# A decoder layer on one core: GpSimd makes the gate's sigmoid and its sum with the experts' bias, behind the second norm's scale

## What is computed

```python
def _moe(x, gate, expert_bias, w1, w2, w3, shared_w1, shared_w2, shared_w3):
    scores = jax.nn.sigmoid((xt @ gate.T).astype(jnp.float32))
    _, sel = jax.lax.top_k(scores + expert_bias[None, :], TOP_K)
    top_scores = jnp.take_along_axis(scores, sel, axis=1) * ROUTE_SCALE
    ...                        # each token times its two scores, through its two experts
    hs = jax.nn.silu(xt @ shared_w1.T) * (xt @ shared_w3.T)
    out = hs @ shared_w2.T
    out = out.at[token_idx].add(out_r)

x = x + _L0_attn_ref(_layernorm(x), ...)                # 16 heads of 16, each token's own heads
x = x + _L0_xattn_ref(_layernorm(x), ctx_2048, ...)     # 16 heads, 2048 keys, fake quantisation
x = x + _L0_ffn_ref(_layernorm(x), ...)                 # 8 experts, the best 2 of each token
```

## Time and profile before

| | |
|---|---|
| median of 3 runs | 1011.39 us (1009.79 to 1011.78) |
| the profiled execution | 1009.28 us, of which the span (first to last instruction) is 1007.5 |
| busy: VectorE, GpSimd, ScalarE, TensorE | 910.5, 748.0, 733.1, 722.3 us |
| mean granted clock of TensorE | 0.859 |
| VectorE's sigmoid L1166, 16 times | 13.2 us |
| VectorE's sum with the bias L1168, 16 times | 27.7 us |
| GpSimd idle ahead of L481, for VectorE's `hs_max` | 52.2 us, 16 times |

### The profile page before, as it was taken

The page is one execution under the profiler, slowest core; times in us unless marked ns, Lnnn a source line. Parts: engine busy times, 40 slices in busy tenths (PEclk is TensorE's granted clock), DMA queues, the critical chain, the costliest instruction groups (busy, mean ns, idle before and its releaser), DMA issues.

```text
span 1007.5 us, 21210 instructions
## 1 busy us (share of the span) xinstructions
PE 722.3 (72%) x7072; PEld 398.6 (40%) x7072; DVE 910.5 (90%) x1841; ACT 733.1 (73%) x989; POOL 748.0 (74%) x728
## 2 busy tenths in 40 slices
PE   6965766777677768687777777686868777777674
PEld 4543222344343434343444434343434444343243
DVE  3896967999999999999999999999999999999942
ACT  2633756878877888787777778788878878787842
POOL 6689988979797979797897979797979889710000
PEclk9986786989997989888888979798988889797955
DMA  6011795999899999999998999999999989999971
GB/s 238 1 43 47 131 168 105 173 153 184 169 183 172 157 174 159 167 173 172 166 173 161 180 157 192 170 158 174 169 158 172 175 163 169 158 195 163 192 147 31
DMA packets 574018, 156.01 MB, mean 155 GB/s; under 512 B 567251, under 2 KB 571862, under 8 KB 573526
## 3 DMA queue, kind: packets, MB, share of 16 engines
q1 hardware_dynamic: 573910, 154.67, 86.7%
HBM read 9.93 MB, written 2.10 MB: 12 GB/s over the span
## 4 chain that ended last, share of the span: by engine, by line
DVE 45%; issue 24%; PE 19%; ACT 4%; DMA 2%; SPq 2%; POOL 2%; DVEq 0%; POOLq 0%; ACTq 0%
DVE score L1134 30%; PE ps_score L1458 7%; PE ps L1316 6%; DVE gate L1168 3%; ACT prob L824 2%; PE ps_score L1316 2%; SPq L423 2%; DVE exp_bias L1144 2%; DVE early L1184 2%; DMA prob_t<-prob 2%; ACT queries L806 1%; DVE gate L1166 1%; DVE q_parts L1117 1%; PE ps_pv L1488 1%; PE ps L1437 1%
## 5 line engine op out<-in xcount | busy, mean ns | idle before, releaser
L1134 DVE TENSOR_SCALAR_CACHE_REDUCE score<-ps_score,q_neg 128x1024 f32<-128x1024 f32 x512 | 636.2, 1278 | 17.0 <-PE ps_score L1458 15.5
L824 ACT ACTIVATE prob<-score,exp_bias 128x2048 uint16<-128x2048 f32 x256 | 511.1, 1997 | 11.6 <-DVE exp_bias L1144 9.3
L1458 PE MATMUL ps_score<-keys,queries 128*128 128x512 bf16 x1024 | 351.8, 444 | 195.0 <-DVE score L1134 156.3
L1458 PEld LDWEIGHTS ps_score<-keys,queries 128*128 128x128 bf16 x1024 | 75.4, 104 | 370.7 <-DVE score L1134 306.0
L527 POOL TENSOR_TENSOR product<-hs_exp,v_tok 128x1024 f32<-128x1024 f32 x64 | 148.5, 2342 | 18.0 <-ACT hs_exp L789 17.9
L534 POOL TENSOR_TENSOR product<-product 128x512 f32<-128x512 f32 x128 | 158.9, 1263 | 0.0
L527 POOL TENSOR_TENSOR product<-qk_rot 128x1024 f32<-128x1024 f32 x64 | 149.6, 2350 | 0.3 <-POOL qk_rot L520 0.2
L545 POOL TENSOR_TENSOR product<-product 128x512 f32<-128x512 f32 x64 | 82.4, 1288 | 5.9 <-POOL product L534 5.9
L877 ACT ACTIVATE routed_both<-normed,routed_gate 128x256 bf16<-128x256 f32 x128 | 57.1, 496 | 37.8 <-DVE routed_gate L1179 37.8
L1488 PE MATMUL ps_pv<-prob_t,values 128*32 128x128 f16 x4096 | 73.0, 227 | 11.0 <-DMA prob_t<-prob 10.9
L1488 PEld LDWEIGHTS ps_pv<-prob_t,values 128*32 128x32 f16 x4096 | 62.0, 101 | 40.4 <-issue 40.4
(11 more groups left out here) (124 smaller groups left out, 1125.8 us busy)
## 6 DMA issues: line engine op xcount, KB each, us to landing
prob_t<-prob SPq DMA_TRANSPOSE x256, 4.7
prob_t<-in_w SPq DMA_DIRECT2D x3, 1024.0 KB, 4.8
x_in<-in_x SPq DMA_DIRECT2D x16, 128.0 KB, 3.1
score<-in_cond_t SPq DMA_DIRECT2D x4, 512.0 KB, 6.6
out<-x_out SPq DMA_DIRECT2D x16, 128.0 KB, 2.5
w_qkv<-in_w_qkv SPq DMA_DIRECT2D x1, 768.0 KB, 4.3
early<-in_w_kv SPq DMA_DIRECT2D x1, 512.0 KB
w_s<-in_w_s SPq DMA_DIRECT2D x3, 128.0 KB
```

What stands on the lines that cost most here:

```text
L824: act.activation(prob[:, s, :].bitcast(U16), score[:, s, :], ACT.Exp, bias=exp_bias[:, s:s + 1], scale=-1.0, accum_out=prob_sum[:, t.par, ...
L1134: dve.tensor_scalar(score[:, s, HALF * i:HALF * i + HALF], ps_score[:, score_slot(t.count(H, h), i)].rearrange("p b k -> p (b k)"), q_neg[ ...
L1458: mm = pe.matmul(ps_score[:, score_slot(n, i), b, :], queries[:, t.par, h // 2, h % 2, :], keys[:, h // 2, k0:k0 + KEYS], start=True, stop ...
```

## The change

Both instructions leave VectorE's `choose`. A new function of GpSimd's, `gate_sums`, makes them: it waits for ScalarE's tanh and, from the second tile on, for the last step of the `choose` before; it makes the sigmoid as a tensor_scalar and the sum as a tensor_tensor (it was a scalar_tensor_tensor). It is called in GpSimd's body directly behind the second norm's `ln_scale(1, n)`. VectorE's `choose` begins with the wait for the second count of `gate_chain`, ahead of `max`. The order of all other instructions stays.

```diff
             def gate_sums(t):
+                sig, biased = gate[:, 0, :], gate[:, 1, :]
+                pool.wait_ge(gate_tanhed, t.count(1, 1))
+                pool.sem_inc(settled, 1)
+                if (due := t.due(6)) is not None:
+                    pool.wait_ge(gate_chain, due)
+                    pool.sem_inc(settled, 1)
+                pool.tensor_scalar(sig, gate_tanh[:], 0.5, 0.5, ALU.mult, ALU.add).then_inc(gate_chain, 1)
+                pool.wait_ge(gate_chain, t.count(6, 1))
+                pool.sem_inc(settled, 1)
+                pool.tensor_tensor(biased, sig, b_expert[:], ALU.add).then_inc(gate_chain, 1)
...
                     ln_scale(1, n)
+                if m.exists():
+                    gate_sums(m)
                 if a.exists():
                     fold_8(0, a)
...
             def choose(t):
-                dve.wait_ge(gate_tanhed, t.count(1, 1))
-                dve.tensor_scalar(sig, gate_tanh[:], 0.5, 0.5, ALU.mult, ALU.add).then_inc(gate_chain, 1)
-                dve.wait_ge(gate_chain, t.count(6, 1))
-                dve.scalar_tensor_tensor(out=biased, in0=sig, scalar=1.0, in1=b_expert[:], op0=ALU.mult, op1=ALU.add
-                                         ).then_inc(gate_chain, 1)
                 dve.wait_ge(gate_chain, t.count(6, 2))
                 dve.max(best, biased).then_inc(gate_chain, 1)
```

More of the change, by code:

```diff
@@ L491, in norm_ho, with gate_sums @@
                 pool.tensor_tensor(ho_n[:], ho[:], over(hs_inv[:], HD), ALU.mult).then_inc(ho_done, 1)
+            def gate_sums(t):
+                sig, biased = gate[:, 0, :], gate[:, 1, :]
[8 more added lines that the diff above has]
+                pool.tensor_tensor(biased, sig, b_expert[:], ALU.add).then_inc(gate_chain, 1)
             def spread_sums(t):
```

## The result

The changed kernel takes 1052.05 us (median of 4 runs, 1048.49 to 1052.93), the kernel before 1011.41 beside it (4 runs, 1009.79 to 1011.78). The ratio is 1.0398, with a 95% interval of 1.0372 to 1.0425: slower by 40.6 us. Forecast were 1048 and a range of 1038 to 1058; the median lies 4 us above the one number and at the upper edge of the stretch 1044 to 1052 that the prediction called the forecast itself. The profiled execution of the changed kernel is the fastest of its four, 1048.49 with a span of 1046.4.

The account below looks back on a forecast made before the run. VectorE was taken to bound the kernel, but would wait for GpSimd's late sums: 1009.3 + 38.3 = 1047.6, with part of the 2.1 us between profiled run and median said as 1048, range 1038 to 1058.

Parts of the forecast that it names:

- What the removed time was: VectorE's two instructions ahead of `max`: 3.49 us per body in bodies 1 to 11, said to be really GpSimd's time.
- The steps on GpSimd: Behind `shift`: 0.08 to the sigmoid, sigmoid 0.23, gap 0.18, sum 0.20, 0.04 to VectorE; `max` 2.21 us later.
- The hold of `routed_gate`: VectorE's `routed_gate`, two SBUF inputs, held until GpSimd's fold ends: the bias 2.65 us later per body instead of 2.21.
- The bias behind `shift`: Head 10's bias on VectorE would start 1.85 us behind the end of GpSimd's `shift`.
- the sum had: Added time over all bodies: 29.2 for bodies 1 to 11, 6.9 for 12 and 13, 2.2 for 14; together 38.3 us.
- Bodies 12 to 14: Last bodies with the second norm: 3.44 us added in each of 12 and 13, 2.2 in body 14.
- Once in every body: GpSimd's wait for `hs_max` lies behind the sums, so its slack can't help; delay paid every body, wait some 5.7 us.
- relief of VectorE: Rival at `choose`: sums ready when VectorE arrives, some 40 us saved, 970; needs GpSimd's 44.7 us run below VectorE's 39.0; chance 0.04.
- No hold: Rival at `routed_gate`: it slips in ahead of GpSimd's fold, 13 x 0.44 less, 1042 us; chance 0.16.
- Slow sums: Rival on GpSimd: add at 0.40 and 0.1 more waiting, 1052 us; at a microsecond each, some 1068; chance 0.08.
- a wait ahead of `shift` that shrank: Rival on GpSimd: it stands earlier in the new rhythm by the 2.65 us lost, so it hardly matters; chance 0.02.
- The rival of TensorE's clock: Rival behind `choose`: longer TensorE stand lowers its clock, VectorE waits 0.5 us more per body for scores, 1054; chance 0.12.

Follow-up runs that it names:

- e3_psum: Kernel before, both sums still on VectorE, with only the gate's tanh and sigmoid placed in PSUM: 976.74 us, ratio 0.9673.
- e7_no_hold: Changed kernel with match_replace's output `marked` in PSUM, so `routed_gate` reads one tensor from SBUF: 1043.11 us, ratio 1.0333 against the kernel before.
- e5: Changed kernel with one extra unused GpSimd add per body behind the sums, at the end of the score folds: 1052.33 us, ratio 1.0413 against the kernel before.
- e4: Changed kernel with one extra unused GpSimd add per body ahead of the second norm's scale and the sums: 1059.12 us, ratio 1.048 against the kernel before.
- e1_early: Changed kernel with the two instructions moved between GpSimd's first two folds, some 5 us ahead of `shift`: 984.92 us, ratio 0.9751 against the kernel before.
- e10: Changed kernel with 36 unused TensorE matmuls per body between the values' product and the scores of head 12: 1051.82 us, ratio 1.041 against the kernel before.
- e2_ahead_of_norm: Changed kernel with the sums directly ahead of the second norm's scale on GpSimd instead of behind it: 1020.02 us, ratio 1.008 against the kernel before.

## Why the prediction was right, point by point

- **What the removed time was**: standing behind GpSimd's instructions, 3.49 us a body. Shown by e3_psum, which takes it away without moving an instruction.
- **Who waits, and for what**: `max` for the sum, 5.4 to 5.6 us idle in bodies 2 to 13, 5.05 in the first, 2.31 in body 14. The text said 14 bodies with some 5.5; it is 13. (The 15th wait of the list, 5.71 in body 16, is one for ScalarE's tanh: before, VectorE itself waited 4.84 for it there.)
- **The steps on GpSimd**: sigmoid 0.20 (0.23 said), gap 0.18, sum 0.20 (0.20 said), 0.03 to VectorE. The 0.08 ahead of the sigmoid, taken from `var_eps`, didn't appear: it started 0.03 before the end of `shift`. So `max` came 0.58 behind `shift` and not 0.73.
- **The hold of `routed_gate`**: 0.60 as said, ending with the fold; e7_no_hold shows the cause and that it is paid.
- **The bias behind `shift`**: 1.71 us (1.12 of it from `max`) where 1.85 was said; from there to the next `hs_max` 11.11 where 11.41 was taken over from before. Together 0.44 less a body than the sum had, some 5.7 in 13 bodies.
- **The period**: 57.27 said, 57.54 measured. So 0.7 a body was added elsewhere. It is a term that the sum lacked: the sum held GpSimd's run from `hs_max` to the end of `shift` at what body 6 showed, 44.01 us (2.53, 20.20 and 21.28 in the table's pieces). Body 6 of the changed kernel has 44.02; the mean of the 13 is 44.71, with 20.75 up to the spreading of the sums as its largest excess, 0.55. The mean of the kernel before was 44.20, so about half a microsecond of it is new.
- **Bodies 12 to 14**: 3.44 each was said for bodies 12 and 13, and their periods grew by 2.94 and 3.30; 2.2 was said for body 14, and 1.36 was added.
- **What was luck**: the steps of the loop are as forecast, but that 38.3 stands so near to the 38.9 of the spans is in part luck. Some 5.7 us too much (the bias and what follows it) and some 9 too little (0.7 a body up to `shift`) cancel for the most part.
- **Once in every body**: GpSimd's wait for `hs_max` grew from 3.78 to 5.45 in body 6 (5.7 said). e5 shows that this slack takes work that stands behind the sums, and e4 that it takes none that stands ahead of them.
- **Rivals**: relief of VectorE (970) didn't come in this place; e1_early, where the sums come early enough, shows that the condition named for it was the right one. No hold didn't occur. Its price, 5.7, fits e7_no_hold, which measured 6.6 by the ratios and 9 by the medians; that 1042 and e7's 1043 lie so near is in part luck, as the forecast that the price was taken from lay 4 us low. Slow sums didn't occur, they took 0.20 each; nor was there a wait ahead of `shift` that shrank, that stretch grew. The rival of TensorE's clock came true in part, in another place than was looked at, and at some 4 us where 6.5 was its price. Behind `choose` it fell to 0.50 as it had before, and the way from the bias to `hs_max` didn't grow (11.11 after 11.34). Behind `hs_max` it is low in six periods and was not before; see below.
- **From the profile to the median**: sum 38.3, difference of the two profiled executions 39.2, difference of the medians 40.6. The profiled execution is the fastest of its four; part of the 2.1 was added for that in the forecast, and all of it would have been nearer.

The half microsecond up to the spreading of the sums is traced as follows. GpSimd waits there for VectorE's reciprocal (`sum_inv`), and VectorE comes later because it waits longer for the first scores of the next tile: summed over the 13 periods, 13.6 us where it was 6.1. The rows over the whole span, before and after:

```profile
L1134 DVE TENSOR_SCALAR_CACHE_REDUCE score<-ps_score,q_neg 128x1024 f32<-128x1024 f32 x512 | 636.2, 1278 | 17.0 <-PE ps_score L1458 15.5
```

```profile
L1149 DVE TENSOR_SCALAR_CACHE_REDUCE score<-ps_score,q_neg 128x1024 f32<-128x1024 f32 x512 | 636.2, 1278 | 22.7 <-PE ps_score L1468 22.4
```

TensorE's low clock lies beside it, and the trace of the changed kernel holds both cases. Two windows of 4 us behind `hs_max`, those of the periods that end in body 6 and in body 7 (same columns as above), and in each the 64 matmuls of the values' product and VectorE's wait for the first scores:

```profile
437.25:441.25 4.00, 2.23 (x74) 1.47 (x74) 3.86 (x13) 3.40 (x6) 1.88 (x2) 1.00 1.27 161
494.07:498.07 4.00, 3.67 (x74) 2.47 (x74) 3.86 (x13) 2.45 (x5) 1.95 (x2) 0.57 1.29 156
```

```profile
437.93 1.08 PE L1498 MATMUL ps_pv<-prob_t,values 128*32 128x128 f16 x64
442.94 1.28 DVE L1149 TENSOR_SCALAR_CACHE_REDUCE score<-ps_score,q_neg 128x1024 f32<-128x1024 f32 x1 [0.15 <-PE ps_score L1468]
...
495.18 1.90 PE L1498 MATMUL ps_pv<-prob_t,values 128*32 128x128 f16 x64
500.65 1.29 DVE L1149 TENSOR_SCALAR_CACHE_REDUCE score<-ps_score,q_neg 128x1024 f32<-128x1024 f32 x1 [1.05 <-PE ps_score L1468]
```

At the lower clock the values' product is longer, the turning of the next queries, which TensorE does behind it, starts 2.94 us behind `hs_max` instead of 2.30, and the first scores come later. Among the periods of bodies 2 to 13, the clock of this window is 0.57 to 0.65 in six and 1.00 in the other six; in the kernel before it is 1.00 in all twelve. The six at the low clock have a mean period of 57.82 us, the others of 57.14, below the 57.27 that was said. So the low clock goes with some 4 us of the whole in this execution. That it is the cause is read from this trace and was shown by no run: e10 left that drop in place. Why the clock falls there in some periods stays open too: in the 2 us ahead of the second window TensorE was busy for 0.61 us, and for 0.60 at the same place of the kernel before (476.09 to 478.09), where the clock stayed at 1.00. Some 0.2 us a body of the wait remain at the full clock, and their cause stays open.

## What to carry to other kernels

Before a step is moved to an engine with time to spare, look at when that engine comes to the step's place in its order against when its reader asks for it: an engine at 74% that comes 5 us late costs more than one at 90% that does the work itself. Two engines that wait for each other once in a period make a loop, and idle time on it helps only on the far side of the wait; an add of half a microsecond on either side tells which side is which. And a small instruction that takes many times its undisturbed length, ending with its neighbour's instruction, is being held by it: try where its operands lie before changing who does it.

## What was not expected of the hardware

Whether GpSimd's work holds an instruction over 128x8 on VectorE depended here on where its operands lie: `routed_gate` took 0.599 us with two inputs in SBUF and 0.166 with one of them in PSUM, the sigmoid 1.159 from SBUF to SBUF and 0.15 from PSUM to PSUM. A GpSimd instruction over one column (`rstd`, 0.57 us) didn't hold it, in 11 bodies before and, with 1.45 us of such steps, in all of e2_ahead_of_norm (at most 0.168). And with matmuls that nothing uses TensorE's granted clock was 1.00 behind `choose` instead of 0.50; the 13 periods became 4.7 us shorter, the end 6.8 us longer, and the median stayed.
